# Reworking the last head pair of an attention and mixture-of-experts kernel

## Chip, core and metric

The kernel runs on one core of a Trainium2 chip. The metric is the device time of one execution in microseconds (us). Before the change it is 820.43 us, the median of three runs (819.67 to 824.2).

## What is computed

Two blocks follow each other, with a residual added after each:

```
x = x + xattn(ctx, latents = layernorm(x), mask)
    q = LN(latents) @ Wq ;  k, v = concat(LN(ctx), LN(latents)) @ Wkv   # 8 heads of 64, q and k of unit length per head
    out = softmax(8 * q k^T + mask) v ;  y = layernorm(out @ Wo)
x = x + ffn(layernorm(x))
    shared = (silu(x w1) * (x w2)) @ w3                          # hidden size 1024
    routed = the two best of 16 experts (hidden size 256), weighted by their sigmoid scores
```

There are 2 batches of 1024 rows of 256 numbers, and 64 rows of context for each batch, so each query has 1088 keys. All arithmetic is in 32-bit floats.

## The kernel before, in words

The order of the work is written out by hand for each engine, with semaphores between them. A name such as `summed` or `o_ready` is a semaphore that counts up.

The attention (stage B) works on 8 head pairs (two heads of one batch), one after the other: `stage_b(i)` in each engine's program. A pair has 18 score slots of up to 128 keys and 512 queries: slots 0 to 8 for the left 512 queries, slots 9 to 17 for the right ones. Slots are scored three at a time in six phases (`SCORED`), and phase f = 3 starts the right half. TensorE makes the scores into PSUM, ScalarE writes their exponentials into one of six `prob` buffers, and TensorE weighs the values with them (`weigh`). The `prob` tile of the shared slot `BOTH` (8) holds half a tile for each side.

The row sums of the softmax are built beside this: GpSimd adds `prob` tiles into `acc` (`add_first`, `add_more`, `add_last`, lines 692 to 710), one half for the left and one for the right queries, each tile 128x1024. VectorE adds two more tiles into `tail` (`add_two`) and GpSimd adds `tail` in at the end of a side. `ADDED` says after which count of `summed` a tile is in, so that ScalarE may write its buffer again. TensorE then sums `acc` over the partitions with a matmul with ones. For pairs 0 to 6 that makes one `sums` bank, ScalarE copies it, and the reciprocals are taken on a spread-out form: SyncE moves the sums into a tile of 16 columns, VectorE inverts it, and it goes to DRAM and comes back repeated over the rows (`spread_sums`, `repeat_rec`, `invert_sums`). For the last pair the two sides are summed apart (`total(14)`, `total(15)`) and VectorE inverts each directly in `divide`, 128x512 at a time. `divide(m)` writes the attention's result `on` and raises `o_ready`.

Stage C is done for 8 tiles t, each of 128 rows of both batches. `project_o(t)` on TensorE multiplies `on` by the output weights into a `y` bank. `stage_c(t)` on VectorE takes statistics (`bn_stats`, `bn_aggr`), scales, adds the residual `xres`, takes statistics again and writes the normalised rows `xf`. GpSimd computes the two inverse deviations of each tile (`deviations_c(t)`) and adds the layer norm's bias to the residual (`add_bias`). SyncE loads the residuals in order (`load_res(t)`): `xres` has two buffers, so tile t waits until tile t - 2 was used. `turn_xf(t)` transposes `xf` on TensorE, ScalarE copies it into `xfT`, and TensorE goes on with the shared hidden units (`hidden`, `down`). The first two tiles stand before the hidden units. `down` of the first unit also waits for `o_ready` 16, so for the right side of the last pair. The product of a hidden unit on VectorE (line 1636) comes after stage C of tile 2 in VectorE's order.

SyncE, like the other engines, takes its instructions in order. A transfer that waits holds up those behind it.

## Time and profile before

| | |
|---|---|
| median of three runs | 820.43 us |
| profiled execution | 816.15 us |
| its span, first to last instruction | 814.4 us |
| TensorE matmuls busy | 794.9 us, 98% |
| VectorE busy | 501.3 us, 62% |
| ScalarE busy | 342.8 us, 42% |
| GpSimd busy | 361.8 us, 44% |

TensorE is busy nearly all the time. In the page's 40 slices of 20.4 us its granted clock is below nine tenths in one slice only:

```profile
PEclk9999999999999999999999989999999999999999
```

The digit 8 is the slice from 468 to 489 us. A 9 stands for 90% or more. The times below are counted in microseconds from the start of the span; the last pair's phase 3 begins near 441 us.

### The profile page before, as it was taken

To read this page: it belongs to the slowest core of one execution; us is meant where nothing else is said; L and a number is where in the kernel's file an instruction comes from. 1 tells how busy PE (TensorE), PEld (TensorE's weight loads), DVE (VectorE), ACT (ScalarE), POOL (GpSimd) and SP (SyncE) were. 2 spreads that over 40 slices of the span, in tenths; PEclk is the share of its full clock that TensorE was granted. 3 is DMA by queue.
4 is the path that set the end of the run, shared out by engine and by line. 5 is a ranking of instruction groups with operands and counts; after the bars stand their busy time and mean duration, and the time that the engine had idled before them with its cause. 6 is when DMAs were issued, how large, how long until landed. Compare 5 with 4: busy or idle time off the path is not lost.

```text
span 814.4 us, 13040 instructions
## 1 busy us (share of the span) xinstructions
PE 794.9 (98%) x4368; PEld 484.8 (60%) x4369; DVE 501.3 (62%) x918; ACT 342.8 (42%) x646; POOL 361.8 (44%) x259
## 2 busy tenths in 40 slices
PE   8999999999999999999999979999999999999998
PEld 4444355554555555455544446766557999999655
DVE  4887867777786878687777376647212333334254
ACT  3555456655655666566555311121111333333110
POOL 2100045858696786858688932301661000000364
PEclk9999999999999999999999989999999999999999
DMA  3105700000100010000020011591522222222243
GB/s 118 40 26 187 233 1 1 2 27 1 29 1 27 1 27 1 7 22 1 27 66 27 14 60 32 163 330 58 188 90 66 91 91 96 90 90 84 78 143 116
DMA packets 52373, 55.99 MB, mean 69 GB/s; under 512 B 8922, under 2 KB 47460, under 8 KB 52324
## 3 DMA queue, kind: packets, MB, share of 16 engines
q1 hardware_dynamic: 49092, 46.82, 18.4%
q0 software_dynamic: 3072, 8.39, 3.2%
q8 instruction: 29, 0.48, 0.2%
q14 instruction: 20, 0.16, 0.1%
q10 hardware_dynamic: 160, 0.14, 0.0%
HBM read 36.60 MB, written 18.67 MB: 68 GB/s over the span
## 4 chain that ended last, share of the span: by engine, by line
PE 88%; issue 4%; POOL 3%; DVE 2%; ACT 2%; DMA 0%; DVEq 0%; POOLq 0%; SPq 0%; ACTq 0%
PE bank L1117 14%; PE bank L933 12%; PE bank L958 11%; PE bank L1182 10%; PE bank L804 10%; PE bank L1132 7%; PE bank L892 6%; PE bank L1191 5%; PE bank L938 4%; PE bank L1024 2%; PE bank L876 2%; POOL acc L704 2%; PE bank L1172 1%; ACT prob L1298 1%; PE bank L953 1%
## 5 line engine op out<-in xcount | busy, mean ns | idle before, releaser
L1298 ACT ACTIVATE prob<-bank,zero 128x512 f32<-128x512 f32 x256 | 160.9, 684 | 75.5 <-PE bank L938 73.0
L1513 DVE TENSOR_REDUCE mx<-bank 128x1 f32<-128x512 f32 x256 | 164.3, 685 | 45.6 <-PE bank L892 44.3
L704 POOL TENSOR_TENSOR acc<-acc,prob 128x1024 f32<-128x1024 f32 (+1 forms) x72 | 179.4, 2492 | 10.3
L958 PE MATMUL bank<-prob,vn 128*64 128x512 f32 x512 | 121.1, 602 | 0.0
L1117 PE MATMUL bank<-xfT,w12s 128*128 128x512 f32 x256 | 117.1, 603 | 0.8 <-ACT xfT L1356 0.8
L766 POOL DMA_INDIRECT slot_result<-slot_results,posi x32 | 31.2, 974 | 160.3 <-DMA slot_results<-yo 148.4
L696 POOL TENSOR_TENSOR acc<-prob 128x1024 f32<-128x1024 f32 x16 | 41.4, 2589 | 118.7 <-ACT prob L1298 97.2
L1182 PE MATMUL bank<-xsT,w_slot 128*128 128x128 f32 x752 | 91.9, 275 | 1.0 <-ACT xsT L1390 1.0
L1182 PEld LDWEIGHTS bank<-xsT,w_slot 128*128 128x128 f32 x752 | 89.2, 191 | 6.0 <-ACT xsT L1390 1.6
L1117 PEld LDWEIGHTS bank<-xfT,w12s 128*128 128x128 f32 x256 | 49.4, 194 | 51.3 <-issue 50.0
L1380 ACT ACTIVATE hidden_units<-bank 128x512 f32<-128x512 f32 x32 | 19.1, 597 | 132.4 <-PE bank L1117 132.4
L958 PEld LDWEIGHTS bank<-prob,vn 128*64 128x64 f32 x512 | 32.2, 136 | 58.8 <-issue 41.1
L938 PE MATMUL bank<-neg_max,ones_r 64*128 64x512 f32 x288 | 58.7, 400 | 3.9 <-DVE neg_max L1533 3.8
L892 PE MATMUL bank<-k_hi,q_hi 64*128 64x512 f32 x256 | 61.5, 475 | 1.0 <-DVE mx L1513 0.8
L933 PE MATMUL bank<-q_hi,k_hi 64*128 64x512 f32 x288 | 62.3, 426 | 0.0
L1132 PE MATMUL bank<-w3s,hidden_units 128*128 128x256 f32 x256 | 61.0, 379 | 0.0
L1804 DVE TENSOR_TENSOR rgT<-hidden_units,bank 128x256 f32<-128x256 f32 x47 | 19.8, 421 | 66.9 <-ACT hidden_units L1395 66.9
L1636 DVE TENSOR_TENSOR hidden_units<-hidden_units,bank 128x512 f32<-128x512 f32 x32 | 21.9, 686 | 59.9 <-ACT hidden_units L1380 59.7
L1132 PEld LDWEIGHTS bank<-w3s,hidden_units 128*128 128x128 f32 x256 | 48.1, 190 | 16.6 <-issue 11.5
L933 PE MATMUL bank<-q_hi,k_lo 64*128 64x512 f32 x288 | 57.5, 391 | 0.0
L933 PE MATMUL bank<-q_lo,k_hi 64*128 64x512 f32 x288 | 57.3, 391 | 0.0
L892 PEld LDWEIGHTS bank<-k_hi,q_hi 64*128 64x128 f32 x256 | 24.5, 183 | 52.6 <-DVE mx L1513 25.6
(173 smaller groups left out, 1122.6 us busy)
## 6 DMA issues: line engine op xcount, KB each, us to landing
w12r<-in_L_ffn_routed_w SPq DMA_DIRECT2D x32, 256.0 KB, 4.1
slot_rows<-zrow SPq DMA_DIRECT2D x47, 128.0 KB, 1.8
xsl<-slot_rows SPq DMA_DIRECT2D x47, 128.0 KB, 2.0
slot_results<-yo SPq DMA_DIRECT2D x47, 128.0 KB, 1.7
w3r<-in_L_ffn_routed_w SPq DMA_DIRECT2D x16, 256.0 KB, 3.5
rec<-row_sum_reciprocals SPq DMA_DIRECT2D x28, 128.0 KB, 2.9
xin<-in_x SPq DMA_DIRECT2D x16, 128.0 KB, 2.0
w12s<-in_L_ffn_shared_w SPq DMA_DIRECT2D x2, 1024.0 KB, 6.7
```

Of the source, the lines that this page charges most:

```text
L696: g.tensor_tensor(acc[:, c, :, :], prob[:, n % PROBS, :, :], prob[:, (n + 1) % PROBS, :, :], ALU.add).then_inc(summed, 1)
L704: g.tensor_tensor(acc[rows, c, :, :], acc[rows, c, :, :], prob[rows, n % PROBS, :, :], ALU.add).then_inc(summed, 1)
L804: last = mm_(dst[:, :], xT_of(n, c)[:, k, :], wqkv[:, k, j * INNER:(j + 1) * INNER], start=(k == 0), stop=(k == DK - 1))
L892: mm_(two[h][:, :], q_hi[p][rows, t * P:(t + 1) * P], k_hi[p][rows, c * QC:(c + 1) * QC], start=True, stop=True).then_inc(ring_made, 1)
L933: mm_(two[h][:, :], lhs[rows, keys], rhs[rows, queries], start=(lhs is k_hi[p] and rhs is q_hi[p]), stop=False)
L938: mm_(two[h][:, :], ones_r[rows, :], neg_max[rows, queries], start=False, stop=True) .then_inc(scores_made, 1)
L958: last = mm_(o_bank(i, c)[rows, :], vn[:, kt, b, (2 * j + h) * DH:(2 * j + h + 1) * DH], prob[:, n % PROBS, h, :], start=(s == 0), stop=(s ...
L1117: last = mm_(hidden_bank(n, w)[:, :], w12s[:, k, w, u * P:(u + 1) * P], xfT[:, k, bass.ds(g * GR, GR)], start=(k == 0), stop=(k == DK - 1))
L1132: last = mm_(bank[4 + j // 2][:, (j % 2) * D:(j % 2 + 1) * D], hbuf[:, u % 4, j * P:(j + 1) * P], w3s[:, u, :], start=(u == 0 and j % 2 == ...
L1182: last = mm_(bank[2 + p][:, j * P:(j + 1) * P], w_slot[:, p, k, j * P:(j + 1) * P], xsT[:, p, k, :], start=(k == 0), stop=(k == DK - 1))
L1298: a(prob[rows, held % PROBS, h, :], bank[2 * (n % 2) + h][rows, :], ACT.Exp, bias=bias[rows, :])\
L1513: v.tensor_reduce(mx[:, h, t, c:c + 1], ring_bank(u)[:, :], AX.X, ALU.max).then_inc(ring_used, 1)
```

## The change

It touches only the last pair and the first tiles of stage C. The sums of the last pair get their own table (`LAST_ADDED`). GpSimd does the left tiles 0 to 5 and the first two right ones. VectorE adds the left `tail` (`add_left`) and the seven other right tiles (`add_right`): four in phase 4, two inside stage C of tile 0, one after it. The left side is summed after phase 3 instead of phase 4; the first and second output projections stand after phases 4 and 5. The right sums go over DRAM as the other pairs' do. GpSimd adds the biases of tiles 0 and 1 before the last pair's first sum, and those of the following tiles only after the rows of the tile before them are normalised.

```diff
+LAST_ADDED = {0: 1, 1: 1, 2: 2, 3: 3, 4: 4, 5: 5, 9: 7, 10: 7, 8: 8, 11: 9, 12: 10, 13: 11, 14: 12, 15: 13, 16: 14}
+LAST_LEFT_SUMMED, LAST_SUMS = 6, 14
 # ring of PSUM banks
-            if i == PAIRS - 1 and f == 4:
-                ring_put("sum", NCH - 2)
-    ring_put("y", 0)
-    ring_put("y", 1)
+            if i == PAIRS - 1 and f >= 3:
+                ring_put(*(("sum", NCH - 2), ("y", 0), ("y", 1))[f - 3])
     ring_put("sum", NCH - 1)
 # SyncE
+        def spread_last():
+            sp.wait_ge(sum_kept, PAIRS)
+            sp.wait_ge(rec_ready, PAIRS - 1)
+            for rows in (LOW, HIGH):
+                sp.dma_start(spread[rows, 0:LAST_COLS], rec[rows.start:rows.start + 1, 0, :]
+                             .rearrange("a (p c) -> a p c", c=LAST_COLS)).then_inc(sum_spread, 16)
+            sp.wait_ge(rec_ready, PAIRS)
+            sp.dma_start(rec_dram[1, 0:2 * QC].rearrange("(p c) -> p c", p=P), spread_rec[:, 0:LAST_COLS])\
+                .then_inc(rec_stored, 16)
+            sp.wait_ge(rec_stored, 16 * PAIRS)
+            for h, rows in enumerate((LOW, HIGH)):
+                sp.dma_start(rec[rows, 1, :], rec_dram[1:2, h * QC:(h + 1) * QC].to_broadcast([DH, QC]))\
+                    .then_inc(rec_loaded, 16)
         load_res(2)
+        spread_last()
         load_res(3)
 # GpSimd
         def deviations_c(t):
             for i in range(2):
                 deviations(cvar_ready, 2 * t + i + 1, crs_ready)
-            if t + 2 < TQ:
-                add_bias(t + 2)
-        for i in range(PAIRS):
+        for i in range(PAIRS - 1):
...
+        pool.wait_ge(c_loaded, 48)
+        add_bias(0)
+        add_bias(1)
+        pool.wait_ge(ring_made, made_to(ring_at[("sums", PAIRS - 2)]))
+        add_first(PAIRS - 1, 0, 0)
+        for s in range(2, 6):
+            add_more(PAIRS - 1, 0, s)
+        pool.wait_ge(summed, SUMS * (PAIRS - 1) + LAST_LEFT_SUMMED)
+        add_first(PAIRS - 1, 1, BOTH + 1)
+        for t in range(2):
+            deviations_c(t)
+        pool.wait_ge(xf_ready, 2)
+        add_bias(2)
+        add_bias(3)
+        deviations_c(EARLY)
         pool.wait_ge(o_ready, NCH)
...
-        for t in range(2, TQ):
-            deviations_c(t)
+        for t in range(EARLY, TQ):
+            if t > EARLY:
+                deviations_c(t)
+            if t + 2 < TQ:
+                pool.wait_ge(xf_ready, t + 1)
+                add_bias(t + 2)
 # TensorE
+            if t == EARLY + 1:
+                pe.wait_ge(sum_kept, PAIRS)
-                if not more and f == 4:
+                if not more and f == 3:
                     total(NCH - 2)
-            if not more:
-                project_o(0)
+                if not more and f > 3:
+                    project_o(f - 4)
-        project_o(1)
         total(NCH - 1)
         project_o(EARLY)
 # ScalarE, after the last exponentials
+        a(rec[:, 0, :], ring_bank(u)[:, :], ACT.Copy).then_inc(sum_kept, 1)
 # VectorE
+        def invert_last():
+            dve.wait_ge(sum_spread, 64 * (PAIRS - 1) + 32)
+            dve.wait_ge(rec_stored, 16 * (PAIRS - 1))
+            v.reciprocal(spread_rec[:, 0:LAST_COLS], spread[:, 0:LAST_COLS]).then_inc(rec_ready, 1)
+        def add_left():
+            v.drain()
+            dve.wait_ge(summed, SUMS * (PAIRS - 1) + LAST_LEFT_SUMMED - 1)
+            v.tensor_tensor(acc[:, 0, :, :], acc[:, 0, :, :], tail[:, :, :], ALU.add).then_inc(summed, 1)
+        def add_right(s, rows=slice(0, P)):
+            n = HELD * (PAIRS - 1) + s
+            v.drain()
+            dve.wait_ge(probs_ready, probs_to(PAIRS - 1, s))
+            dve.wait_ge(summed, SUMS * (PAIRS - 1) + LAST_ADDED[s] - 1)
+            v.tensor_tensor(acc[rows, 1, :, :], acc[rows, 1, :, :], prob[rows, n % PROBS, :, :], ALU.add).then_inc(summed, 1)
...
                         add_both(i)
+                        if not more:
+                            add_left()
-                if f == 4 and i:
+                if f == 3 and not more:
                     divide(2 * i - 1)
-                if f == 5:
-                    if more:
-                        negate(0)
-                    else:
-                        v.drain()
-                        divide(NCH - 2)
+                    v.drain()
+                    divide(NCH - 2)
+                if f == 4 and more and i:
+                    divide(2 * i - 1)
+                if f == 4 and not more:
+                    add_right(BOTH, HIGH)
+                    for s in range(BOTH + 3, BOTH + 6):
+                        add_right(s)
+                if f == 5 and more:
+                    negate(0)
                     add_two(i, BOTH + 7, LEFT_SUMMED)
...
-        stage_c(0)
+        stage_c(0, (BOTH + 6, BOTH + 7))
+        add_right(BOTH + 8)
         stage_c(1)
+        invert_last()
+        stage_c(EARLY)
         divide(NCH - 1)
         v.drain()
-        stage_c(EARLY)
```

`divide(15)` takes the reciprocals from the loaded `rec` and the product from the bank. `stage_c` puts the first of its extra additions after the scaled `yn`, the second after its second statistics.

TensorE, last pair, from the weighing of the shared slot (L953 before, L985 after) on; `acc,ones_r` is the sum of a side, `wo_sb,on` an output projection. Before:

```order
L953 MATMUL bank5<-prob,vn 64x512 x2
L933 MATMUL bank0<-q_hi1,k_hi1 128x512 [waits probs_ready]
L933 MATMUL bank1<-q_hi1,k_hi1 128x512
...
L958 MATMUL bank5<-prob,vn 64x512 [waits probs_ready]
L958 MATMUL bank5<-prob,vn 64x512
L978 MATMUL bank6<-acc,ones_r 64x512 [waits summed,ring_used]
L978 MATMUL bank6<-acc,ones_r 64x512
L933 MATMUL bank2<-q_hi1,k_hi1 128x512 [waits probs_ready]
```

After:

```order
L985 MATMUL bank5<-prob,vn 64x512 x2
L1010 MATMUL bank6<-acc,ones_r 64x512 [waits summed,ring_used]
L1010 MATMUL bank6<-acc,ones_r 64x512
L965 MATMUL bank0<-q_hi1,k_hi1 128x512 [waits probs_ready]
...
L990 MATMUL bank5<-prob,vn 64x512
L1058 MATMUL bank7<-wo_sb,on 128x256 [waits ring_used,o_ready,c_loaded]
L1058 MATMUL bank7<-wo_sb,on 128x256 x7
L965 MATMUL bank2<-q_hi1,k_hi1 128x512 [waits probs_ready]
```

The sum of the left side moved ahead of three score slots, and the first projection took its place.

SyncE, from the first part of the shared third weights `w3s` on; `spread`, `row_sum_reciprocals` and `rec` are the way over DRAM, `xres` the residual loads. Before:

```order
L558 DMA w3s<-in_L0_ffn_shared_w3 128x2x256 [waits o_ready]
L550 DMA xres<-in_x 128x256 [waits xres_used]
L550 DMA xres<-in_x 128x256
L550 DMA xres<-in_x 128x256 [waits xres_used]
L550 DMA xres<-in_x 128x256
L563 DMA w3s<-in_L0_ffn_shared_w3 128x6x256 [waits o_ready]
```

After:

```order
L555 DMA xres<-in_x 128x256 [waits xres_used]
L555 DMA xres<-in_x 128x256
L566 DMA spread<-rec 64x1x8 [waits rec_ready,sum_kept]
L566 DMA spread<-rec 64x1x8
L569 DMA row_sum_reciprocals<-spread_rec 128x8 [waits rec_ready]
L573 DMA rec<-row_sum_reciprocals 64x512 [waits rec_stored]
L573 DMA rec<-row_sum_reciprocals 64x512
L555 DMA xres<-in_x 128x256 [waits xres_used]
L555 DMA xres<-in_x 128x256
L584 DMA w3s<-in_L0_ffn_shared_w3 128x6x256 [waits o_ready]
```

Five transfers with three waits stand between the residual of tile 2 and that of tile 3.

GpSimd, the deviations (`sd`, `rs`) and biases (`xres<-xres,lno`) of stage C. After the change (before it, a bias stood behind every second pair of `sd` and `rs`):

```order
L666 TENSOR_TENSOR sd<-mv,eps 128x2 [waits cvar_ready]
L668 TENSOR_TENSOR rs<-sd,half 128x2
L704 TENSOR_TENSOR xres<-xres,lno 128x512 [waits xres_loaded0,xf_ready]
L704 TENSOR_TENSOR xres<-xres,lno 128x512 [waits xres_loaded1]
L666 TENSOR_TENSOR sd<-mv,eps 128x2 [waits cvar_ready]
```

The biases of tiles 2 and 3 both stand ahead of the first deviations of tile 2.

## Rows read from the trace of the kernel before

**Rows 1.** TensorE in order of time: start, us, what, [idle before, releaser].

```profile
446.31 1.09 PE L953 MATMUL bank<-prob,vn 64*64 64x512 f32 x8
...
454.36 1.08 PE L978 MATMUL bank<-acc,ones_r 128*64 128x512 f32 x4 [1.77 <-POOL acc L710]
...
471.45 1.08 PE L978 MATMUL bank<-acc,ones_r 128*64 128x512 f32 x4
...
476.02 0.60 PE L1069 MATMUL bank<-ident,xf 128*128 128x128 f32 x4
480.79 1.11 PE L1069 MATMUL bank<-ident,xf 128*128 128x128 f32 x4 [4.17 <-DVE xf L1438]
482.68 9.50 PE L1117 MATMUL bank<-xfT,w12s 128*128 128x512 f32 x16 [0.78 <-ACT xfT L1356]
...
495.48 1.03 PE L1132 MATMUL bank<-w3s,hidden_units 128*128 128x256 f32 x4
...
497.64 3.60 PE L1117 MATMUL bank<-xfT,w12s 128*128 128x512 f32 x8
...
505.39 0.60 PE L1069 MATMUL bank<-ident,xf 128*128 128x128 f32 x4
```

**Rows 2.** Stretches: busy us of each engine, then PEclk, DMA share, GB/s.

```profile
450.00:455.00 5.00, 3.23 (x20) 1.12 (x16) 0.00 (x0) 2.32 (x4) 4.71 (x3) 1.00 0.00 0
...
480.00:485.00 5.00, 3.43 (x7) 1.89 (x8) 4.83 (x4) 1.88 (x2) 0.76 (x3) 0.57 0.00 0
485.00:490.00 5.00, 5.00 (x10) 2.08 (x9) 3.62 (x12) 0.60 (x1) 2.16 (x11) 0.75 0.59 185
```

**Rows 3.** GpSimd in order of time.

```profile
427.15 2.40 POOL L696 TENSOR_TENSOR acc<-prob 128x1024 f32<-128x1024 f32 x1 [3.08 <-PE bank L969]
...
439.57 5.22 POOL L683 TENSOR_TENSOR xres<-xres,lno 128x512 f32<-128x512 f32 x2
...
491.99 1.27 POOL L683 TENSOR_TENSOR xres<-xres,lno 128x512 f32<-128x512 f32 x1 [1.37 <-DMA xres<-in_x]
```

**Rows 4.** Line 1542, all its instructions: duration in ns min/median/max, starts, forms.

```profile
L1542 DVE TENSOR_TENSOR tail<-prob x16: 1209/1509/2893, 125.5 to 461.0; 128x1024 f32<-128x1024 f32 x16
```

**Rows 5.** VectorE in order of time.

```profile
455.48 3.36 DVE L1558 RECIPROCAL rec<-bank 128x512 f32<-128x512 f32 x1 [10.14 <-PE bank L978]
458.91 0.69 DVE L1566 TENSOR_TENSOR on<-bank,rec 128x512 f32<-128x512 f32 x1
...
484.86 0.76 DVE L1428 BATCH_NORM_STATS2 st<-bank 128x6 f32<-128x256 f32 x2
...
487.47 0.88 DVE L1661 SCALAR_TENSOR_TENSOR x<-yn,rs,xres 128x256 f32<-128x256 f32 x2 [0.56 <-POOL rs L647]
...
490.65 0.74 DVE L1438 TENSOR_SCALAR xf<-x,mv,rs 128x256 f32<-128x256 f32 x2 [1.14 <-POOL rs L647]
```

**Rows 6.** ScalarE: its copy of the sums of the pair before.

```profile
427.11 0.60 ACT L1306 ACTIVATE rec<-bank 128x512 f32<-128x512 f32 x1 [0.42 <-PE bank L969]
```

**Rows 7.** SyncE's queue, order of issue, the pair before: start, us, what.

```profile
427.73 2.44 SPq L523 DMA_DIRECT2D spread<-rec  x4
431.61 0.33 SPq L529 DMA_DIRECT2D row_sum_reciprocals<-spread_rec  x1
433.43 2.41 SPq L534 DMA_DIRECT2D rec<-row_sum_reciprocals  x4
```

**Rows 8.** Landings of lines 523 (spread), 529 (store), 534 (repeat), 550 (residual).

```profile
DMA to landing us min/median/max: 1.6/1.7/2.8
DMA to landing us min/median/max: 1.4/1.4/3.1
DMA to landing us min/median/max: 2.8/2.9/3.2
DMA to landing us min/median/max: 1.9/2.2/4.6
```

**Rows 9.** DMA issues by line: KB each, median us to landing.

```profile
w3s<-in_L_ffn_shared_w SPq DMA_DIRECT2D x1, 768.0 KB, 4.8
```

More of the change, by code:

```diff
@@ L304, in place_rounds, with added @@
         return [(i + 1, r) for r in NEXT_ROUNDS[f][a]] if i + 1 < PAIRS else []
+    def added(i):
+        return ADDED if i + 1 < PAIRS else LAST_ADDED
     def probs_to(i, k):
@@ L423, in build @@
     QROWS = P // (2 * CH)
+    LAST_COLS = QC // DH
     GB = NG - 1
@@ L702, in add_more @@
             pool.wait_ge(probs_ready, probs_to(i, s))
-            pool.wait_ge(summed, SUMS * i + ADDED[s] - 1)
+            pool.wait_ge(summed, SUMS * i + added(i)[s] - 1)
             g.tensor_tensor(acc[rows, c, :, :], acc[rows, c, :, :], prob[rows, n % PROBS, :, :], ALU.add).then_inc(summed, 1)
@@ L717, in _ @@
                 add_more(i, 0, s)
-            if i == PAIRS - 1:
-                pool.wait_ge(c_loaded, 48)
-                add_bias(0)
-                add_bias(1)
             add_first(i, 1, BOTH + 1)
@@ L727, in _ @@
             add_last(i, 1, TAILS, SUMS)
-        deviations_c(0)
-        deviations_c(1)
+        pool.wait_ge(c_loaded, 48)
[13 more added lines that the diff above has]
+        deviations_c(EARLY)
         pool.wait_ge(o_ready, NCH)
@@ L975, in total @@
             dst = ring_slot("sum", m)
-            pe.wait_ge(summed, SUMS * (PAIRS - 1) + (LEFT_SUMMED, SUMS)[m % CH])
+            pe.wait_ge(summed, SUMS * (PAIRS - 1) + (LAST_LEFT_SUMMED, LAST_SUMS)[m % CH])
             for h, rows in enumerate((LOW, HIGH)):
@@ L1287, in exponentials @@
                 j, k = divmod(old, HELD)
-                if k in ADDED:
-                    act.wait_ge(summed, SUMS * j + ADDED[k])
+                if k in added(j):
+                    act.wait_ge(summed, SUMS * j + added(j)[k])
                 if k in TAIL_ADDED:
@@ L1348, in _ @@
             stage_b(i)
+        u = ring_at[("sum", NCH - 1)]
+        act.wait_ge(ring_made, made_to(u))
+        act.wait_ge(o_ready, NCH - 1)
+        a(rec[:, 0, :], ring_bank(u)[:, :], ACT.Copy).then_inc(sum_kept, 1)
         def copy_xfT(t):
@@ L1554, in divide @@
             b, j = divmod(i, PAIRS // B)
-            if m >= NCH - 2:
+            if m == NCH - 2:
                 u = ring_at[("sum", m)]
@@ L1562, in divide @@
             else:
-                dve.wait_ge(rec_loaded, 64 * (i + 1))
-                dve.wait_ge(o_kept, m + 1)
-                o = o_raw[:, c, :]
+                dve.wait_ge(rec_loaded, 64 * (i + 1) if i + 1 < PAIRS else 64 * i + 32)
+                if i + 1 < PAIRS:
+                    dve.wait_ge(o_kept, m + 1)
+                    o = o_raw[:, c, :]
+                else:
+                    dve.wait_ge(pv_done, HELD * (i + 1))
+                    o = o_bank(i, c)[:, :]
             v.tensor_tensor(on[:, 4 * c:4 * c + 4, b, j * P:(j + 1) * P], o.rearrange("p (t q) -> p t q", q=P),
@@ L1647, in add_shared, with stage_c @@
             v.drain()
-        def stage_c(t):
+        def stage_c(t, meanwhile=()):
+            meanwhile = list(meanwhile)
             y = lambda c: y_bank(t)[:, c * D:(c + 1) * D]
@@ L1656, in stage_c @@
             last.then_inc(y_used, 1)
+            for s in meanwhile[:1]:
+                add_right(s)
             v.drain()
@@ L1666, in stage_c @@
             variances(x2_, cvar_ready)
+            for s in meanwhile[1:]:
+                add_right(s)
             dve.wait_ge(crs_ready, 2 * t + 2)
             normalise(lambda c: xf[:, 2 * t + c, :], x2_, xf_ready)
-        stage_c(0)
+        stage_c(0, (BOTH + 6, BOTH + 7))
+        add_right(BOTH + 8)
         stage_c(1)
+        invert_last()
+        stage_c(EARLY)
         divide(NCH - 1)
         v.drain()
-        stage_c(EARLY)
         hid = 0
```

## The prediction

> **What bounds the kernel now.** I read the busy table and the 40 slices first: TensorE is busy almost throughout, so only its idle time and its clock can be won. Then TensorE's own order of time around the end of the attention. It shows two places where it stands still. It waits 1.77 us for GpSimd's last left addition before it sums the left half of the last pair (start 454.36), and 4.17 us for the normalised rows of the second output tile before it transposes them at 480.79; a wait of 0.78 us for ScalarE's copy follows [rows 1]. The stretches of 5 us show what the long wait costs beside itself: the granted clock is 1.00 in 450 to 455, the stretch that holds the 1.77 us wait, and 0.57 and 0.75 in the two stretches that follow the 4.17 us wait, which is the lower level (1.2 GHz) for part of each [rows 2]. Sixteen matmuls of the first hidden units take 9.50 us from 482.68, where eight take 3.60 later (3.43 each further eight, 6.9 for sixteen) [rows 1]. So the fall costs 2.5 to 2.6 us. After that TensorE waits for nothing longer than a microsecond. What can be won is 1.77 + 4.17 + 2.5 plus half a microsecond of transposes at the low clock: 9.0 us. The question is what ends last at each of these places once it is gone.
>
> **Step 1: left sums.** The last "both" weighing begins at 446.31 and is over at 447.3 [rows 1]. GpSimd's five left sums are ready at 439.57, where it now turns to its two biases (5.22 us), which delays all right additions [rows 3]. After the change the biases come before the pair, into the 3.08 us in which GpSimd waits for the sums bank before 427.15 [rows 3]. A bias takes 1.27 us alone (at 491.99) and 2.6 beside a VectorE addition (at 439.57) [rows 3]. There VectorE reduces PSUM tiles and GpSimd kept its pace, so I take 2.6 for both together and no delay; at 2.6 each GpSimd would be 2.1 us late, at 441.7, and still be before VectorE's tail addition ends (443.0). Cost nil at both ends. The left tail addition moves to VectorE, which has it at 443.1. A 128x1024 addition of two SBUF operands took 1.21 us at best and 2.89 at worst [rows 4]; GpSimd waits for this one, so I take 1.21: ready at 444.4, at worst 446.0. TensorE asks at 447.3: the 1.77 us are gone. VectorE's reciprocal (3.36) then runs 448.4 to 451.8 and the product (0.69) ends at 452.5 [rows 5].
>
> **Step 2: output tiles beside the scores.** The same matmuls stand in another order, so TensorE reaches every later point 1.77 us sooner unless it waits. The first projection is asked for at 453.5 (447.3 + 1.0 sum + 5.2 of score and weighing matmuls), its operand is there at 452.5: one microsecond of slack. It ends at 457.2. The second ends at 466.9. The right sum starts at 471.45 - 1.77 = 469.7 and ends at T = 470.7; the third projection ends at 476.02 - 1.77 = 474.25 [rows 1].
>
> **Step 3: VectorE adds.** Seven right additions move to it: four between 452.6 and stage C of tile 0, two inside that stage, one behind it. GpSimd is idle beside the first four, so each is 1.21 + 0.1 for the drain: 457.8. A stage C takes 6.5 us from its first statistics at 484.86 to the last normalise, which starts at 490.65 and takes 0.74 [rows 5]. Part of that is waiting for GpSimd's small operations (1.14 us each time), under which the two inner additions fit but for their own length; at worst they add it whole: 457.8 + 6.5 + 2.6 + 1.3 = 468.2. The right sum asks at 469.7, no wait, 1.5 us to spare. Tile 1 starts then and is normalised by 468.2 + 6.5 = 474.7; its transposes are asked for at 474.25 + 0.45 = 474.7. So the 4.17 us wait is gone, with no slack to speak of. Two transposes and two copies later (0.6 each) the hidden units start at 476.1; full clock, 6.9: 483.0; the fourth projection: 486.5. Before, the down projection behind it began at 495.48 [rows 1]. That is the whole 9.0 us.
>
> In VectorE's rows an addition with GpSimd at work ranges from 1.21 to 2.89 us [rows 4], and a bias took 2.6 or 1.27 [rows 3]. The Trainium skill ("SBUF — State Buffer", on the shared port pair) calls the pair an exclusive lock: whoever starts first holds it for the whole instruction. The rows fit that: at 439.57 the two biases took 5.22 us while VectorE had its tail addition. By that rule GpSimd's small operation behind the second statistics of tile 0 would wait a whole addition, 1.2 us, before it starts; the sum above holds that length already.
>
> **Step 4: the last sums over DRAM.** VectorE saves a 3.36 us reciprocal. In its place stand a ScalarE copy (0.60), two spreading transfers, a small reciprocal, a store, and two repeating loads, all but the last step ahead of the residual load of tile 3 in SyncE's order. And GpSimd adds the bias of tile 3 before it makes the deviations of tile 2. So tile 2 now waits for the residual of tile 3, which waits for the round trip. Priced from the pair before [rows 6, 7]: copy ends at 471.3; from first spreading issue to store issue 431.61 - 427.73 = 3.88 with four transfers, 2.66 with two: 474.0; store to first repeat 433.43 - 431.61 = 1.82: 475.8; two repeats issued at 0.6 each: 477.0; the residual's second transfer goes out near 477.5 and lands 2.2 later, or a little more behind the repeats: 480.0. Bias 1.27: 481.3. Deviations 1.14: 482.5. VectorE's add in tile 2 then starts at 482.6; before it was at 487.47, and 3.92 later the tile was normalised [rows 5]: 486.5. The product with the reciprocals (0.7) comes next, 487.2, and only behind it the first hidden product (0.7): 488.0. TensorE wants that at 486.5. A new wait of 1.5 us, and 7.5 us are left of the 9.0. Bounds from the transfers' own extremes [rows 8]: nothing (the residual 1.5 us sooner) and 5.2 us more (1.1 + 1.7 + 2.4, repeats aside).
>
> The Trainium skill ("DMA: Bandwidth & Descriptors", on the anatomy of one DMA) puts a fixed cost of about 2 us on each transfer (for GpSimd's path). The rows show 1.7 and 1.4 for the small ones [rows 8]. By the page the chain would be some 0.9 us longer, an estimate, and the result by as much.
>
> **Step 5: once more for tile 4.** The big weight load waits for the product (487.2), takes 4.8 to land [rows 9], and the residual of tile 4 is right behind it: 492.2, bounds 490.4 and 493. Then its bias, 493.5, which now stands ahead of the deviations of tile 3; the add of tile 3 starts at 494.7, and the tile is normalised at 498.6. TensorE asks for it at 505.39 - 7.5 = 497.9 [rows 1]. That is 0.7 us more (0 to 1.2). Before, the bias at 491.99 was in good time [rows 3]. From there the round of residual load, bias, deviations and add takes about 7 us against TensorE's 9 for a tile, so nothing grows. Everything later hangs on TensorE and moves with it.
>
> **Sum.** 9.0 - 1.5 - 0.7 = 6.8 us. The profiled execution took 816.15 (span 814.4); it becomes 809.4. The median of the timed runs stands 4.3 above the profiled one; I subtract the same from it: 820.4 - 6.8 = 813.6 us.
>
> **Rivals.**
> A, all slack holds and the round trip is hidden: gain 9.0, 811.4. For it: the fastest landings are not much below the medians, so it needs the residual to slip ahead. Chance 0.07.
> B, the new gap at 486.5 brings the clock down as the 4.17 us one did: another 2.5 lost, gain 4.3, 816.1. Against it, 1.77 us did not [rows 2], and this one is 1.5; for it, a second wait at 498 follows. Chance 0.17.
> C, the wait only moves: the transfers of step 4 land at their longest, 5.2 us more. The new gap is then 6.7 us, longer than the one that lowered the clock, so 2.5 go too: 6.8 - 5.2 - 2.5 = -0.9, or 821.3. Against it: maxima of 28 and 16 issues, all at once. Half of the 5.2 would leave about 4 us. Chance 0.10.
> D, slower: VectorE's seven additions run at the slow 2.89 us. Step by step that is 7 x 1.68 = 11.8 us more, less 1.5 of slack, so the right sum ends 10.3 us late, and steps 4 and 5 with it: 6.8 - 10.3 = 3.5 slower, 823.9. It decides from 2.4 us an addition (7 x 1.2 = 8.3, less 1.5). For it are the long additions of [rows 4]; against it, those lie beside GpSimd's additions, which are gone here. Chance 0.08.
>
> **How the numbers follow.** The forecast has 0.58. What this kernel's measurement can tell from no change is about 0.5%, 4.1 us. Faster: forecast 0.58, A 0.07, most of B 0.10, in all 0.75. Same: the rest of B 0.07 and C 0.10, 0.17. Slower: 0.08. The forecast's own range is 811 to 816; with B and the milder half of C, and the spread of the runs (819.67 to 824.2), the range is 810.8 to 818.5.
>
> **What would show it.** Right: no wait of TensorE for the left sum; the first projection beside the scores; transposes of tile 1 near 474.7 with at most half a microsecond of wait, and the sixteen matmuls behind them in 7 us with clock 1.00; a wait of 1 to 3 us for the first hidden product near 486.5, which leads back over the bias of tile 3 to its residual load and the spreading transfers; additions of 1.2 us on VectorE. Wrong: additions above 2 us; a clock of 0.50 anywhere there; the wait gone (I have mispriced the round trip) or above 4 us.

## The result and the profile after

The changed kernel takes 817.95 us, the median of 10 runs (816.47 to 821.61); before takes 822.78 beside it (10 runs, 819.35 to 827.83). The ratio is 0.9949, with an interval of 0.9926 to 0.9973: 4.2 us gained, between 2.2 and 6.1. (The ratios here are the recorded ones, not quotients of the medians; those two lie 4.8 us apart.) Forecast were 6.8. The profiled execution took 817.73 us (span 816.0) and before's 816.15 (span 814.4), so these two differ the other way; the late pause described below explains it.

TensorE around the last pair, in order of time (start, duration, line, output and inputs, count, the wait ahead and who ended it). This execution reaches the last pair 0.4 us later than the one of before:

```profile
447.69 1.08 PE L1010 MATMUL bank<-acc,ones_r 128*64 128x512 f32 x4
...
453.90 3.72 PE L1058 MATMUL bank<-wo_sb,on 128*128 128x256 f32 x16
...
469.90 1.03 PE L1010 MATMUL bank<-acc,ones_r 128*64 128x512 f32 x4
470.86 3.72 PE L1058 MATMUL bank<-wo_sb,on 128*128 128x256 f32 x16
474.42 1.04 PE L1102 MATMUL bank<-ident,xf 128*128 128x128 f32 x8
476.29 7.10 PE L1150 MATMUL bank<-xfT,w12s 128*128 128x512 f32 x16 [0.83 <-ACT xfT L1392]
483.23 3.62 PE L1058 MATMUL bank<-wo_sb,on 128*128 128x256 f32 x16
489.62 1.71 PE L1165 MATMUL bank<-w3s,hidden_units 128*128 128x256 f32 x4 [2.77 <-DVE hidden_units L1702]
491.12 1.06 PE L1102 MATMUL bank<-ident,xf 128*128 128x128 f32 x4
491.97 1.75 PE L1165 MATMUL bank<-w3s,hidden_units 128*128 128x256 f32 x4
493.56 3.60 PE L1150 MATMUL bank<-xfT,w12s 128*128 128x512 f32 x8
```

Both long waits of [rows 1] are gone, and the sixteen matmuls take 7.10 us instead of 9.50. In their place stands one wait of 2.77 us. Busy time and granted clock (the column behind POOL busy) by stretches of 5 us:

```profile
480.00:485.00 5.00, 5.00 (x17) 2.89 (x16) 1.01 (x3) 1.19 (x2) 2.12 (x3) 1.00 0.02 5
485.00:490.00 5.00, 2.23 (x11) 1.65 (x10) 3.33 (x9) 0.00 (x0) 2.06 (x9) 1.00 0.03 6
490.00:495.00 5.00, 5.00 (x16) 3.62 (x15) 1.96 (x7) 0.60 (x1) 0.83 (x1) 0.66 0.60 205
```

The clock is 1.00 where [rows 2] had 0.57 and 0.75, but now falls to the lower level (1.2 GHz) for part of 490 to 495. From the first down projection to the hidden units behind it 3.94 us go by (489.62 to 493.56), where before took 2.16 (495.48 to 497.64) [rows 1]: 1.8 us.

What the wait leads back to, in rows of SyncE's queue, GpSimd and VectorE in turn:

```profile
471.60 1.13 SPq L566 DMA_DIRECT2D spread<-rec  x2
474.70 0.33 SPq L569 DMA_DIRECT2D row_sum_reciprocals<-spread_rec  x1
476.15 1.10 SPq L573 DMA_DIRECT2D rec<-row_sum_reciprocals  x2
477.29 1.06 SPq L555 DMA_DIRECT2D xres<-in_x  x2
```
```profile
481.53 1.26 POOL L704 TENSOR_TENSOR xres<-xres,lno 128x512 f32<-128x512 f32 x1 [5.63 <-DMA xres<-in_x]
482.76 0.20 POOL L666 TENSOR_TENSOR sd<-mv,eps 128x2 f32<-128x2 f32 x1
```
```profile
457.26 1.23 DVE L1633 TENSOR_TENSOR acc<-acc,prob 128x1024 f32<-128x1024 f32 x1 [0.16 <-DVE acc L1633]
...
483.90 0.88 DVE L1730 SCALAR_TENSOR_TENSOR x<-yn,rs,xres 128x256 f32<-128x256 f32 x2 [7.22 <-POOL rs L668]
...
488.88 1.28 DVE L1702 TENSOR_TENSOR hidden_units<-hidden_units,bank 128x512 f32<-128x512 f32 x2 [0.45 <-issue]
```

That is the chain of step 4. VectorE's seven additions took 1.22 or 1.23 us each.

Near the end the profile shows something that none of the rows of before had (TensorE, then ScalarE):

```profile
789.58 3.60 PE L1150 MATMUL bank<-xfT,w12s 128*128 128x512 f32 x8
795.82 2.44 PE L1165 MATMUL bank<-w3s,hidden_units 128*128 128x256 f32 x8 [2.65 <-DVE hidden_units L1702]
```
```profile
782.89 0.60 ACT L1416 ACTIVATE hidden_units<-bank 128x512 f32<-128x512 f32 x1 [4.56 <-issue]
794.45 1.08 ACT L1416 ACTIVATE hidden_units<-bank 128x512 f32<-128x512 f32 x2 [10.96 <-PE bank L1150]
```

ScalarE normally takes a hidden unit every 5.16 us (4.56 idle, 0.60 of work). Here it skips one and takes two together at 794.45, TensorE waits 2.65 us and its clock falls for 3.4 us. I call it the late pause; its cost is 4.6 us (at 789.58 the kernel is 4.1 ahead of before, at its last matmul 0.5 behind).

### The profile page after: what moved, and what is told of

It reads as the page before. It is cut to its first block, busy times and chain, and to the rows that moved or that the text cites. A ratio compares the mean times of both kernels' runs of the same rounds, so it can differ in the third digit from the quotient of the medians.

```text
span 816.0 us, 13063 instructions
## 1 busy us (share of the span) xinstructions
PE 796.0 (98%) x4368; PEld 486.3 (60%) x4369; DVE 500.2 (61%) x925; ACT 343.7 (42%) x647; POOL 342.4 (42%) x252
## 4 chain that ended last, share of the span: by engine, by line
PE 88%; issue 6%; DVE 2%; ACT 2%; POOL 1%; DMA 0%; POOLq 0%; ACTq 0%; DVEq 0%
PE bank L1150 13%; PE bank L965 12%; PE bank L990 11%; PE bank L836 11%; PE bank L1215 10%; PE bank L1165 7%; PE bank L924 6%; PE bank L1224 5%; PE bank L970 4%; PE bank L1058 2%; PE bank L908 2%; ACT prob L1331 1%; PE bank L1205 1%; PE bank L985 1%; PE bank L1001 1%
## 5 line engine op out<-in xcount | busy, mean ns | idle before, releaser
L723 POOL TENSOR_TENSOR acc<-acc,prob 128x1024 f32<-128x1024 f32 (+1 forms) x67 | 166.8, 2490 | 9.6
L1165 PE MATMUL bank<-w3s,hidden_units 128*128 128x256 f32 x256 | 62.9, 388 | 5.4 <-DVE hidden_units L1702 5.4
```

What stands on the lines that cost most here:

```text
L723: g.tensor_tensor(acc[rows, c, :, :], acc[rows, c, :, :], prob[rows, n % PROBS, :, :], ALU.add).then_inc(summed, 1)
L1165: last = mm_(bank[4 + j // 2][:, (j % 2) * D:(j % 2 + 1) * D], hbuf[:, u % 4, j * P:(j + 1) * P], w3s[:, u, :], start=(u == 0 and j % 2 == ...
```

## Experiments

Gains inside a span are taken between profiles at the first expert slot's matmuls (line 1215, in before 1182; 623.18 in before, 619.11 after), net of when each execution reached the last pair. By that measure the changed kernel's first profile is 4.4 us ahead of before's. Run 4 says 5.5, run 9 3.8 against run 11, run 14 5.3 against run 13.

**Run 1, residual first.** SyncE only:

```diff
         load_res(2)
-        spread_last()
         load_res(3)
+        spread_last()
```


> The changed kernel with SyncE's residual load of tile 3 put ahead of the round trip of the last sums; nothing else. Theory 1 (the new wait of 2.77 us for the first hidden product is the chain spreading transfers, residual of tile 3, its bias, the deviations of tile 2, and it lowers the clock for 3.4 us): the bias of tile 3 starts by 476, VectorE's add in tile 2 by 477.5 instead of 483.9, TensorE begins the down projection near 486.9 without a wait at clock 1.00, 4.5 us less than the changed kernel (about 813.4, 1.0% under the kernel before). Theory 2 (VectorE's product with the reciprocals, which waits for the repeated sums, ends last as well): the wait stays above 2 us although GpSimd is early, and the time is that of the changed kernel. Theory 3 (what is missing to the forecast was lost in the last 60 us of the program): the wait goes, the time hardly does.

816.96 us against 822.21 of before, ratio 0.9929 (0.9901 to 0.9957). No wait at the first down projection and clock 1.00 there. Two pauses of 1.75 us much earlier (line 924, at 225 and 362 us) hide it in this span; net of them the first slot is where run 2's is, 4.7 us ahead of the changed kernel's.

**Run 2, deviations first.** GpSimd only:

```diff
         add_bias(2)
-        add_bias(3)
         deviations_c(EARLY)
+        add_bias(3)
```


> The changed kernel with GpSimd's deviations of tile 2 ahead of its bias of tile 3; the transfers stay as they are, so the residual of tile 3 still lands at 481.5. Theory 1: that residual costs nothing when no deviation stands behind it, the first product comes near 482, no wait of TensorE, 4.5 us less than the changed kernel. Theory 2: the wait stays. If only SyncE's order mattered and not GpSimd's, this kernel would be as the changed one.

815.8 us, ratio 0.9923 (0.9891 to 0.9955). The wait is gone, the first slot comes at 613.94, which is 9.1 us sooner than in before.

**Run 3, direct reciprocal.** `spread_last`, ScalarE's copy and `invert_last` are left out; VectorE divides the last sums directly, ahead of tile 2 (and TensorE waits for the first part of the shared third weights ahead of the last sum):

```diff
-        invert_last()
-        stage_c(EARLY)
         divide(NCH - 1)
         v.drain()
+        stage_c(EARLY)
```


> The changed kernel without the round trip: VectorE inverts the last sums directly (3.36 us) between tiles 1 and 2 as the kernel before does, ScalarE's copy and the five transfers are left out, the wait for the first part of the shared third weights stands ahead of the last sum. Theory 1: VectorE starts tile 2 4.1 us later than now (478.8), so the scaled rows of tile 2 are 4 us later and the second hidden unit waits about 1 us for their bank near 480; the first product is done near 486, before it is asked for: 3.5 us less than the changed kernel. If the round trip is what pays in the change, this kernel is slower than the changed one by up to 3.4 us.

815.02 us, ratio 0.9915 (0.9885 to 0.9945). The wait moved and shrank: 0.84 us in the middle of the sixteen matmuls (at 479.89, for VectorE's line 1716), no fall of the clock, first slot 614.6. That is 3.6 us ahead of the changed kernel and 1.1 us behind run 2: the way over DRAM gains about 1 us over a plain reciprocal, and only when nothing queues behind it.

**Run 4, the changed kernel again**, on the chip of runs 1 to 3.

> The changed kernel itself once more, for the spread of its executions. Theory 1: ratio 0.995 to the kernel before as found, the wait for the first hidden product again 2.5 to 3 us and the clock 0.50 behind it. The pause of ScalarE of 6.4 us near 788 in the first profile is not of the change and stands elsewhere or is missing.

817.82 us, ratio 0.9955 (0.9932 to 0.9977). The wait was 2.56 us and the clock stayed at 1.00 through it, where 0.50 was expected. In its place stands a second, short wait, for the rows of tile 3, which the first profile does not have:

```profile
498.75 1.03 PE L1165 MATMUL bank<-w3s,hidden_units 128*128 128x256 f32 x4
500.33 0.66 PE L1102 MATMUL bank<-ident,xf 128*128 128x128 f32 x4 [0.55 <-DVE xf L1474]
```

Runs 1 to 3 beat it by 0.9 to 2.8 us in the medians, with intervals that overlap. All four profiles had the late pause.

**Runs 5 and 8, before again**, on another chip (before's median there 815.94).

> The kernel before once more, one profile. Five of five profiles of the changed kernel and its variants show a pause near 790, 19 us before the end: the first of two hidden units is finished, ScalarE takes it up 6.4 us late, TensorE then waits 2.6 us and the clock is 0.50 for 3.4 us, 4.6 us in all. The first profile of the kernel before has none. Theory 1: the pause belongs to both kernels and its absence in that one profile was luck (816.15 us against a median of 822): this profile has it, at about the same distance from the end. Theory 2: the change brings it about: this profile has none, and the change gives back 4.6 us of its gain there.

> The kernel before a third time, one profile, for the same question as the second: is the pause of ScalarE near 790 there or not, and where else do its executions lose the 4 to 6 us by which the median of the timed ones lies above the first profile. Theory 1: there.

816.52 and 816.63 us, no late pause in either; waits of 1.76 to 1.77 and 4.12 to 4.15 us as in [rows 1]. So the pause is not something that every profile of every kernel has; but chip and kernel changed together here, so these two runs cannot say which of the two brings it.

**Run 6, GpSimd adds.** The seven right additions and their tail back on GpSimd; all else as changed:

```diff
         add_first(PAIRS - 1, 1, BOTH + 1)
+        add_more(PAIRS - 1, 1, BOTH, HIGH)
+        for s in range(BOTH + 3, BOTH + 7):
+            add_more(PAIRS - 1, 1, s)
+        add_last(PAIRS - 1, 1, TAILS, LAST_SUMS)
```


> The changed kernel with the right additions of the last pair back on GpSimd (one tail addition of two tiles on VectorE as before); all else as changed. Theory 1: GpSimd is busy with them until about 468 and makes the first deviations of stage C only then, tile 1 is normalised near 480.5, TensorE waits 5 to 5.5 us for it at 475 and the clock falls; the hidden units start near 482 instead of 476.3 and the program is about 3 to 4 us slower than the changed kernel. Rival: GpSimd's deviations are not what holds stage C, the start of the hidden units stays within 1 us.

814.59 us, ratio 0.9981 (0.9967 to 0.9995). TensorE's waits in that stretch:

```profile
476.96 1.12 PE L1106 MATMUL bank<-ident,xf 128*128 128x128 f32 x4 [3.07 <-DVE xf L1478]
478.85 9.12 PE L1154 MATMUL bank<-xfT,w12s 128*128 128x512 f32 x16 [0.78 <-ACT xfT L1396]
```

The wait for the left sum is gone, but the second long wait of before stays, 3.07 instead of 4.17 us, with its fall of the clock for 6.8 us. The wait is shorter than the 5 to 5.5 us expected; the first slot is 1.7 us ahead of before's, 2.8 to 3.9 behind the changed kernel's.

**Run 7, projections late.** The first two output projections back behind phase 5 and behind the last weighing.

> The changed kernel with the first two output projections back behind phase 5 and behind the last weighing; left sum and additions as changed. Theory 1: stage C of tile 0 starts at 463.7 instead of 458.7, tile 1 is normalised near 480, the wait of TensorE before its transposes is 5 us again with the low clock behind it, the hidden units start near 482. Rival: VectorE's stage C has slack, and the wait is under 1 us.

818.06 us, ratio 1.0021 (1.0007 to 1.0035): slower than before. The hidden units start at 481.54, as expected (482), but the wait stands elsewhere, ahead of the last sum: VectorE's additions, behind tile 0, now end last:

```profile
473.42 1.08 PE L1012 MATMUL bank<-acc,ones_r 128*64 128x512 f32 x4 [3.67 <-DVE acc L1636]
...
494.82 1.71 PE L1168 MATMUL bank<-w3s,hidden_units 128*128 128x256 f32 x4 [2.73 <-DVE hidden_units L1705]
```

By the ratios, the projections moved without the additions leave a gain of 1.6 us, no more than the wait of 1.77 us that the earlier left sum takes away in both runs, and the additions moved without the projections lose 1.7. Neither move pays without the other.

**Runs 9 to 12, one chip for both kernels** (before 816.09 us). Run 10 joins the edits of runs 1 and 2; run 12 is run 2 again.

> The changed kernel once more, for the pause some 19 us before its end (TensorE waits 2.6 us at a down projection for a hidden unit that ScalarE had taken up late, and the clock then falls for 3.4 us). It stood in all five profiles of kernels with VectorE's additions taken so far and in none of five of the other kernels, but those came from another chip. Theory 1, the pause belongs to the changed kernel: it stands here too, whatever before shows in this batch, and the ratio to before is about 0.995. Theory 2, it belongs to the chip or to chance: this profile and the one of before have it or lack it alike; where both lack it, the changed kernel's span is 811.5 (816.0 less 4.6) and the ratio about 0.993 (4.1 to 5.4 us gained).

> Both of the reorderings at once: SP issues tile 3's residual ahead of the round trip of the last sums, and GpSimd works tile 2's deviations ahead of tile 3's bias. Theory of the queue (each of the two already takes away the whole wait of 2.6 to 2.8 us before the first down projection): no wait and no fall of the clock there, first down projection at 486 to 487, first expert slot 9.2 us earlier than in before, and no gain over one of them alone (within 0.5 us). Rival (the residual moved ahead holds up the round trip, whose last projection is next in line): the first down projection at 487.5 to 488.5. Ratio to before 0.989 without the late pause, 0.992 with it.

> Before, unchanged, on the chip of this batch: does it show the pause some 19 us before the end? Theory 1 (the pause belongs to the changed kernel): no pause, span about 814.9. Theory 2 (it belongs to the chip): the pause is here if it is in the changed kernel's profiles of this batch, with a span of about 819.5.

> GpSimd works tile 2's deviations ahead of tile 3's bias; SP's order as in the changed kernel. First expert slot 9.2 us earlier than in before, as in its first run. Theory 1 (the late pause belongs to the kernels with the additions on VectorE): the pause is there and the span is 810.6, the ratio 0.992. Theory 2 (chip or chance): as in before's profile of this batch; where before has none, the span is 806.0 and the ratio 0.989.

| run | median | ratio to before | span | wait at the first down projection |
|---|---|---|---|---|
| 9, changed | 813.6 | 0.9960 (0.9946 to 0.9975) | 811.7 | 2.70, clock falls 3.4 us |
| 10, both orders | 808.19 | 0.9891 (0.9871 to 0.9911) | 808.4 | none |
| 11, before | 815.72 (one run) | | 814.0 | none (4.07 earlier) |
| 12, deviations first | 809.55 | 0.9911 (0.9892 to 0.9930) | 806.6 | none |

None of the four has the late pause. Run 12's TensorE, where the changed kernel waits:

```profile
483.02 3.62 PE L1058 MATMUL bank<-wo_sb,on 128*128 128x256 f32 x16
486.48 1.03 PE L1165 MATMUL bank<-w3s,hidden_units 128*128 128x256 f32 x4
```

Against run 11 it begins the down projection 8.4 us sooner (net) and keeps all of it. Run 10 gains nothing over one of its two edits: its first slot, net of a pause of 1.75 us early on, is where run 12's is. The 1.4 us between their medians are within the spread.

**Runs 13 to 16**, a fourth chip (before 818.24 us).

> Before once more, to see the late pause of 4.6 us beside the changed kernel's on the same chip. If the pause belongs to the chip: it is here exactly if it is in r14. If it belongs to the changed kernel on some chips only: here never, whatever r14 shows. Span 814 to 815 without it, about 819 with it.

> The changed kernel beside r13. Span 811 to 812 without the late pause, 815 to 816 with it. The wait before the first down projection is 2.5 to 2.8 us again on any chip, since it comes from the order of the queues; the clock falls there for 3.4 us or not at all (it did at 2.77 and 2.70, not at 2.56).

> The changed kernel with the biases of tiles 0 and 1 back between GpSimd's left and right additions of the last pair. Theory: the right additions are VectorE's now, so GpSimd has 7 us to spare there; the two biases end at 442.5, or at 445 if they share the SBUF port with VectorE's left tail addition, which then ends at 444.7 to 446; TensorE asks at 447.7: no wait, ratio to the changed kernel 1.000 (within 0.5 us). Rival: the port delays VectorE's tail addition past 447.7: a wait of up to 1.5 us for the left sum.

> Both reorderings again. Ratio to before 0.989 as in its first run if neither kernel, or both, show the late pause on this chip; 0.993 to 0.995 if it is the changed order's own and shows up here.

Run 13 took 820.87 and run 14 825.15 us; no late pause in any of the four. Both had the pauses of 1.75 us (line 924, in before 892), a wait of TensorE for VectorE's `k_lo`: two in run 13, five in run 14, two of those with a fall of the clock. Pauses and falls bring run 14 to the last pair 12.6 us later than the first profile, so a single execution can differ by that much for them alone. What makes them come is open. Run 14 waited 2.99 us for the first hidden unit with the clock at 1.00, and 0.57 us for tile 3 as run 4 did. Run 16: 809.1 us, ratio 0.9885 (0.9833 to 0.9938), no wait. Run 15 moves `add_bias(0)` and `add_bias(1)` back between GpSimd's additions: 813.89 us, ratio 0.9938 (0.9905 to 0.9970), the left sum still without a wait, though the two do collide (GpSimd, then VectorE):

```profile
441.19 4.60 POOL L704 TENSOR_TENSOR xres<-xres,lno 128x512 f32<-128x512 f32 x2
```
```profile
444.74 2.13 DVE L1625 TENSOR_TENSOR acc<-acc,tail 128x1024 f32<-128x1024 f32 x1
```

The place of the first two biases is worth nothing once the additions are VectorE's: the hidden units start as soon behind the last pair as in the changed kernel (29.60 us behind the weighing of the shared slot, there 29.62). The wait for the first hidden unit was 3.10 us in this profile, with a fall of the clock for 6.8 us.

**Runs 17 and 18, the length of VectorE's code.** The program ends 3.4 us behind TensorE's last matmul in all five profiles of before and in run 6, but 4.2 to 4.6 us behind it in the changed kernel and in runs 1 to 4, 7, 9, 10, 12 and 14 to 16. In the DMA view these have 21 packets on the second instruction queue (runs 10 and 14 have 22), the others 20 (queue, packets, MB, share), before first:

```profile
q14 instruction: 20, 0.16, 0.1%
```
```profile
q14 instruction: 21, 0.17, 0.1%
```

The one more comes after the last matmul (after, 811.5 to 816 us, and SyncE's wait for the last output, 1.7 us in before):

```profile
q14 instruction: 1, 0.01, 1.0%
```
```profile
SPq L638 <- DMA out<-x: 2.7, 1, 2.7
```

The kernels divide by the number of VectorE's instructions in the built program: 1198 in before and 1201 in run 6, 1219 (run 3) and 1220 in the others. Run 17 gives before 22 drains more where VectorE is idle, run 18 gives the version of run 10 forty:

```diff
+        for _ in range(22):
+            v.drain()
         for t in range(TQ):
             dve.wait_ge(x_loaded, ...
```


> Before, with 22 drains more in VectorE's code, at a place near the start where VectorE is idle for 5 us, so that its code is as long as the changed kernel's (1220 instructions, 1198 in before). Theory (the end of VectorE's code comes to lie behind one more block of instructions, which is fetched only when VectorE gets there): 21 packets of the second instruction queue instead of 20, the last 1.9 us behind TensorE's last matmul, and a program end 4.2 to 4.6 us behind that matmul instead of 3.38; ratio to before 1.001. Rival (the later end has to do with the changed order of work, say the state of the output transfers): 20 packets, 3.38 us, ratio 1.000.

> The version with both reorderings, with 40 drains more at the same place (1260 VectorE instructions). Theory: the border of the block moves some 40 instructions ahead, out of the program's end into code that VectorE passes earlier, so the last packet comes before TensorE's last matmul and the end is 3.4 us behind it, 1.0 us sooner than in the version without drains: ratio to before 0.988. Rival: any longer code keeps the late fetch: 4.4 us again.

Run 17, before's own order of work, has 21 packets, the last some 2.8 us behind the last matmul, and ends 4.94 us behind it, more than the 4.2 to 4.6 expected. Run 18 also has 21, but the last one comes between 775 and 785 us, and it ends 3.39 us behind the last matmul. SyncE's last wait in run 17, then in run 18:

```profile
SPq L617 <- DMA out<-x: 2.6, 1, 2.6
```
```profile
SPq L638 <- DMA out<-x: 1.7, 1, 1.7
```

So the microsecond belongs to the code's length: drains alone bring it (run 17) and take it away (run 18). The Trainium skill ("Runtime: NRT & Kernel Launch", table of terms) says that an engine's instruction memory is refilled in blocks of 16 KiB. By the rows, the first instruction queue moves 0.48 MB in 29 packets, which agrees; the second moves 0.16 MB in 20, so about 8 KB each, half of that. The times of these two runs cannot show 1 us: 821.48 us, ratio 1.0007 (0.9991 to 1.0022), and 813.39 us, ratio 0.9899 (0.9875 to 0.9922).

Run 17 bears on the late pause too. It has it, in before's order:

```profile
799.67 1.56 PE L1132 MATMUL bank<-w3s,hidden_units 128*128 128x256 f32 x6 [2.64 <-DVE hidden_units L1638]
```

By chip: there in all six profiles from two chips (runs 1 to 4, 17 and 18), in none of twelve from three others, whatever the kernel. Before's medians on the two are 822.21 and 821.22 us, on the other three 815.94, 816.09 and 818.24. So it goes with the chip a kernel runs on, or with something else that its batch of runs shared, and not with the change. For the first comparison the chips are not on record: the changed kernel's profile has the pause, before's has none, and before's timed runs (822.78) are as long as on the chips with it.

What makes ScalarE skip a turn is open; no run tried it. One thing marks the place: the hidden unit that ScalarE takes late is the one behind which a packet of the first instruction queue follows by 2.3 to 2.8 us, in five profiles without the pause (before: unit at 792.14, packet at 794.4; runs 9, 11, 12, 14) as in five with it (after: 794.45 and 796.8; runs 2, 4, 17, 18). The fetching of code is a candidate that nothing here confirms or rules out.

## Why the forecast was too large

**Step 1: right.** The left sum starts at 447.69 without a wait, the biases fit into GpSimd's gap; run 15 shows that even this was not needed.

**Step 2: right.** First projection at 453.90 (forecast 453.5), third at 470.86 with its end at 474.4 (474.25).

**Step 3: right.** Additions of 1.22 us, transposes at 474.42 without a wait, hidden units at 476.29 at the full clock. Rival D is out: nothing slowed them. Run 6 shows that without them 3.07 of the 4.17 us stay. The term of 9.0 us for this stretch measured 9.1 in run 2 and 8.4 in run 12 against run 11.

**Step 4: the term that failed.** The mechanism is shown: take either link away (runs 1 and 2) and the wait is gone. Its size was wrong, 2.56 to 2.99 us in the four profiles of the changed kernel instead of 1.5. Issues ran about as forecast up to the first repeat (476.15 for 475.8), but the residual's second transfer went out near 477.8 and the bias could start only at 481.53, not at 480.0; VectorE's drain ahead of the hidden product took 0.45 more. I had priced the residual's landing, which stood right behind the repeats, at hardly more than its median of 2.2 us; it took some 3.7.

The runs show that the repeats ahead of it make the difference, not a dearer transfer. The same load of tile 3, two transfers of 128 KB, behind the two repeats of 128 KB (first profile) and ahead of the round trip (run 1), in KB and median us to landing:

```profile
xres<-in_x SPq DMA_DIRECT2D x2, 128.0 KB, 3.1
```
```profile
xres<-in_x SPq DMA_DIRECT2D x2, 128.0 KB, 2.1
```

The 3.1 us are 2.6 for the first transfer and 3.6 for the second, which the bias waits for. The median is 3.0 to 3.4 us in runs 2, 4, 9, 12 and 14, which have the same order of transfers, and 2.1 us in runs 3, 10 and 16, where no repeat is ahead of it. By the Trainium skill's fixed 2 us for a transfer ("DMA: Bandwidth & Descriptors", anatomy of one DMA) the wait would have been 2.4 us, nearer than mine, but for another reason: the small transfers still landed in 1.7 and 1.4 us. The store was issued 3.10 us behind the first spreading transfer where I had 2.66, because VectorE's small reciprocal stood behind the normalised rows of tile 1 and began at 474.48.

The longer wait also did what rival B says: it lowered the clock in the first profile and in run 9, for 1.8 us. B, given 0.17, came to pass in those two. It is no certainty, since 2.56 and 2.99 us left the clock at 1.00. B's number, 4.3 us gained, is close to the measured 4.2, but by luck: B is made of a wait of 1.5, a fall of 2.5 and the 0.7 of step 5, and lacks the missing term below.

By the first slot, and against run 2 or 12, the changed kernel is 4.7 us (first profile), 3.6 (run 4), 4.6 (run 9) and 4.1 (run 14) behind. In the first and third that is the wait and the fall of the clock, in the other two the wait and step 5. Forecast were 2.2 for both steps. Run 12 against run 9, on one chip, says 4.1 by the medians and 5.1 by the spans (4.5 net of a start 0.6 sooner).

**Step 5: right where the clock stayed up.** In runs 4 and 14 TensorE waits 0.55 and 0.57 us for tile 3, and falls back by 0.8 us there; 0.7 was forecast. In the first profile and run 9 tile 3 is transposed (at 501.32 in the first) without a wait, since the fall of the clock had held TensorE back by 1.8 us. So the fall costs only about 1 us more than a run in which it stays away.

**A term that was missing: 1.0 us** for one more block of VectorE's code, fetched behind the last matmul (runs 17 and 18).

**The base.** I subtracted the gain from medians that stood 4.3 us above the profile. The late pause would explain that: the profile of before has none, and on the chips with it before's medians are 3 to 6 us longer. The first comparison's two profiles differ in it, so their spans say nothing of the change. That 817.95 lies in the stated range of 810.8 to 818.5 says little either: 6.8 us off the 822.78 measured beside it would have been 816.0. Taken between runs 11 and 9, the spans say 2.3 us, or 2.8 net of a start 0.5 later: 8.4 of waits and clock, less 2.7 for the new wait, 1.8 for the fall of the clock and 1.0 for the code, which makes 2.9. The three comparisons have ratios of 0.9949, 0.9955 and 0.9960, or 3.3 to 4.2 us. Rival A is out as it was put (the round trip is not hidden), but its 9.0 us are what run 10's order gives: 0.9891 is 8.9 us (7.3 to 10.5). Rival C is out: landings were late by one microsecond, not five.

The best version is that of run 10: both reorderings, 808.19 and 809.1 us where before has 816.09 and 818.24. The forty drains of run 18 should take another 1.0 us off it; that was seen in where the program ends, not in a time.

## What to carry to other kernels

When a change puts a new chain ahead of something that already waits in an in-order queue, ask whether the queued item needs the chain at all: exchanging two lines (the deviations of the tile at hand before the bias of the next) was worth as much as the whole change. Price a transfer by what stands right ahead of it in its queue (here 2.1 us with nothing, 3.0 to 3.4 behind two of its size), and let the fall of the clock into the forecast once the wait comes near 3 us, less what it hides of the waits behind it. Compare the tails of two profiles as well as their middles: a pause of one chip and a block of code can each move the end by more than the edit does.

## What the hardware showed that I had not expected

- A fall of TensorE's clock after a wait of about 3 us is not certain. Of waits in the middle of the program 2.56 and 2.99 us left it at 1.00; 2.70, 2.73, 2.77 and 3.67 lowered it for 3.4 us; 3.07, 3.10 and 4.07 to 4.17 for 6.8 us. The wait of the late pause, 2.58 to 2.65 us, lowered it in six of seven profiles and left it at 1.00 in run 17 (2.64 us). Even 1.75 us lowered it twice in run 14 and once in run 18, while 1.77 us never did in the six profiles of before's order.
- 22 drains in idle time at the start of VectorE's program put the end 1.6 us further behind the last matmul (4.94 for 3.38), and 40 in a longer version brought it back to 3.39.
- Two of five chips add a pause of 2.6 us at one place, which ends 19 to 20 us before the program does, in every profile taken there. It costs 4.3 to 4.6 us with a fall of the clock behind it, and 2.9 without one (run 17).
- GpSimd's small power operation took 1.57 us at 464.71 beside a VectorE addition and 0.69 to 0.71 otherwise. That is longer by about what was left of the addition (464.50 to 465.73), as the rule in the prediction has it. VectorE's addition took 2.13 beside GpSimd's biases (run 15) and 1.22 otherwise.
